# Ten chunks of several lists started after 17 routed tiles, and the chunk table computed in two parts

## The reference, cut to what matters

```python
def _moe(tokens, router_w, w1, b1, w2, b2):       # N=3125, D=256, E=8, TOP_K=2
    logits = tokens.astype(jnp.float32) @ router_w.astype(jnp.float32).T
    probs = jax.nn.softmax(logits, axis=-1)
    rw, re = jax.lax.top_k(probs, TOP_K)
    if TOP_K > 1:
        rw = rw / jnp.maximum(rw.sum(-1, keepdims=True), 1e-12)
    combine = jnp.zeros((N, E), tokens.dtype).at[jnp.arange(N)[:, None], re].set(rw)
    out = tokens
    for e in range(E):
        h = jax.nn.gelu(tokens @ w1[e] + b1[e], approximate=False)
        y = h @ w2[e] + b2[e]
        out = out + combine[:, e:e + 1] * y
    return out
...
x = x + _L0_gnn_ref(xn, src, dst, ...) + _L0_mix_ref(xn[None], ...)[0]
x = x + _L0_ffn_ref(_layernorm(x, axis=-1)[None], ...)[0]
```

## Time and profile before

| | |
|---|---|
| median of 3 runs | 435.66 (435.45, 435.66, 439.13) |
| profiled execution, own time | 435.45 |
| its span (first to last instruction) | 433.4 |
| outside the span | 2.05 |
| PE / DVE / ACT / POOL busy share of the span | 92% / 74% / 62% / 49% |
| mean granted TensorE clock | 0.976 of 2.4 GHz |

### The profile page before, as it was taken

One profiled execution on the slowest core, in us unless ns is written; L12 is line 12 of the kernel. 1 busy time (PEld: TensorE's weight loads), 2 busy tenths in 40 slices (PEclk: granted clock), 3 DMA queues, 4 the chain that ended last, 5 costly groups with the idle time before them and its releaser, 6 DMA issues.

```text
span 433.4 us, 10046 instructions
## 1 busy us (share of the span) xinstructions
PE 400.3 (92%) x3131; PEld 315.7 (73%) x3131; DVE 319.6 (74%) x785; ACT 269.5 (62%) x676; POOL 212.6 (49%) x298
## 2 busy tenths in 40 slices
PE   1989899997999999999999999778999999899995
PEld 0878687876777777777765667563999999788994
DVE  3587959968899999999916842677688887645653
ACT  1756555576788788888834525440767676566663
POOL 4124768258334455544410024365356655655565
PEclk9999999999999999999999969877999999999999
DMA  8937210007499899999997781123466665476761
GB/s 211 190 81 257 73 27 4 3 2 151 82 176 170 160 166 162 175 166 176 169 177 279 242 283 63 43 96 112 147 180 207 188 205 155 125 189 195 201 190 43
DMA packets 111828, 64.11 MB, mean 148 GB/s; under 512 B 87986, under 2 KB 102203, under 8 KB 111647
## 3 DMA queue, kind: packets, MB, share of 16 engines
q1 hardware_dynamic: 104590, 48.14, 50.4%
q0 software_dynamic: 6368, 14.47, 9.7%
q10 hardware_dynamic: 816, 0.85, 0.8%
HBM read 24.00 MB, written 21.44 MB: 105 GB/s over the span
## 4 chain that ended last, share of the span: by engine, by line
PE 40%; DVE 26%; issue 12%; POOL 7%; DMA 7%; ACT 3%; DVEq 2%; SPq 1%; POOLq 0%
PE bank L1420 5%; DVE region_c L1132 5%; DVE region_a L980 5%; PE bank L1432 4%; PE bank L1370 4%; PE bank L1463 4%; PE bank L1335 3%; DVE region_a L1293 3%; PE bank L1344 2%; PE bank L1669 2%; DVE region_a L1287 2%; POOL out L651 2%; PE bank L1680 2%; DMA out<-region_a 2%; PE bank L1582 2%
## 5 line engine op out<-in xcount | busy, mean ns | idle before, releaser
L716 ACT CAST region_a<-bank 128x500 bf16<-128x500 f32 (+1 forms) x119 | 72.4, 670 | 15.7 <-PE bank L1370 14.7
L1669 PE MATMUL bank<-region_a,region_c 128*128 128x128 f32 x496 | 65.6, 275 | 0.0
L1680 PE MATMUL bank<-region_c,region_a 128*128 128x256 f32 x248 | 64.0, 380 | 0.0
L1669 PEld LDWEIGHTS bank<-region_a,region_c 128*128 128x128 f32 x496 | 60.3, 192 | 0.1
L1132 DVE COPY region_c<-region_w 128x1026 f32 x62 | 43.2, 697 | 18.8 <-issue 18.0
L986 DVE TENSOR_TENSOR region_a<-iota,locs 128x3200 bf16<-128x3200 bf16 x25 | 54.6, 2182 | 0.0
L1370 PE MATMUL bank<-region_a 128*128 128x125 bf16 x625 | 52.9, 219 | 1.5 <-ACT region_a L716 1.4
L1370 PEld LDWEIGHTS bank<-region_a 128*128 128x128 bf16 x625 | 42.2, 101 | 13.5 <-ACT region_a L716 3.2
L625 POOL DMA_INDIRECT xs<-rows,slot_i x25 | 24.7, 989 | 53.8 <-ACT rows L760 36.7
L980 DVE TENSOR_TENSOR region_a<-iota,keys 128x3150 bf16<-128x3150 bf16 x25 | 47.5, 1900 | 0.5 <-PE bank L1370 0.4
L601 POOL TENSOR_TENSOR rows<-rows,bp 125x256 f32<-125x256 f32 x25 | 46.6, 1866 | 0.0
(11 more groups left out here) (239 smaller groups left out, 780.1 us busy)
## 6 DMA issues: line engine op xcount, KB each, us to landing
region_a<-xs_next SPq DMA_DIRECT2D x31, 259.0 KB, 2.9
region_w<-in_w SPq DMA_DIRECT2D x4, 1024.0 KB, 9.9
region_a<-xs SPq DMA_DIRECT2D x31, 131.0 KB, 2.3
rows<-in_x SPq DMA_DIRECT2D x5, 560.0 KB
xs_next<-null SPq DMA_DIRECT2D x8, 259.0 KB, 3.8
xs_next<-null SPq DMA_DIRECT2D x1, 1554.0 KB, 10.7
xs<-null SPq DMA_DIRECT2D x8, 131.0 KB, 2.7
region_q<-in_b SPq DMA_DIRECT2D x1, 1024.0 KB, 9.7
```

The source lines that it names most:

```text
L716: nc.scalar.copy(to, count_bank(n)[:, 0:w * TP].rearrange("p (c t u) -> p c t u", c=w, t=NT)).then_inc(adj_done, 1)
L1669: last = nc.tensor.matmul(hid_ps[c % 2][:, f * P:(f + 1) * P], wc[:, c % 3, k * D + f * P:k * D + (f + 1) * P], xT[:, c % 2, k * P:(k + 1) ...
L1680: last = nc.tensor.matmul(y_ps[c % 2][:, 0:D], hT[:, c % 2, f * P:(f + 1) * P], wc[:, c % 3, (2 + f) * D:(3 + f) * D], start=False, stop=( ...
```

## The change

1. The chunks that are given out early are ten instead of three, known after 17 tiles (`SURE_T`) instead of 22, and they are whole chunks of whichever lists hold them, in the order of the lists: 17 x 125 rows less 7 x 127 that may stand in part chunks leave at least ten whole ones. `whole_chunks` divides the counts by 128 behind `weigh(3)`; `sure_chunks` turns them into rows and experts behind `choose(4)`, ahead of `weigh(4)`.
2. SP waits for the scatters of 17 tiles before the first ten loads, for the first part of the table before chunks 10 to 30, and for the second part before chunks 31 to 61.
3. PE's 26 filling matmuls and the wait for 22 scatters are gone; `positions` of the last group moves behind the loop, directly ahead of `turn_rows(0)`.
4. DVE copies the weights of chunks 0 and 1 behind `weigh(4)`, of chunk 2 behind `choose(5)`, of chunk 3 behind the weighting of chunk 0.
5. The table is split by role. Part one is begun before and finished behind the weighting of chunk 0; part two is spread over seven steps behind the weighting of chunks 12 to 18 (`SECOND` = 12).
6. The two weights of a row are made by POOL (`row_weights`, behind `goals`) instead of DVE (L1290).
7. `xch` moves to its own place in `region_q`, behind `b2x`; the second result bank is `spare` instead of `h1`.

The diff, cut to the parts named here:

```diff
-SURE = -(-ROUT[-1][0] * TP // (NX - 1)) // P
+SURE_G = 3
+SECOND = 12
+SURE_T = ROUT[SURE_G][1]
+SURE = -(-(SURE_T * TP - (NX - 1) * (P - 1)) // P)
...
-        xt_ps, hid_ps, y_ps = (y0, y1), (m0, m1), (h0, h1)
+        xt_ps, hid_ps, y_ps = (y0, y1), (m0, m1), (h0, spare)
...
-            sp.wait_ge(sent, ROUT[-1][0] * 16)
+            sp.wait_ge(sent, SURE_T * 16)
             for c in range(SURE):
                 load_chunk(c)
             sp.wait_ge(table_done, 1)
-            sp.wait_ge(sent_last, (NT - ROUT[-1][0]) * 16)
-            for c in range(SURE, NCH):
+            sp.wait_ge(sent_last, (NT - SURE_T) * 16)
+            for c in range(SURE, MC):
+                load_chunk(c)
+            sp.wait_ge(table_done, 2)
+            for c in range(MC, NCH):
                 load_chunk(c)
...
+            def row_weights(c):
+                pool.wait_ge(turned_gap, c + 1)
+                nc.gpsimd.tensor_scalar(xch[:, c % XB, W_LOW:W_HIGH + 1], halves[:], turn[:, c:c + 1], 0.5, ALU.mult,
+                                        ALU.add).then_inc(weights_made, 1)
...
             goals(0)
+            row_weights(0)
             for c in range(MC):
                 if c + 1 < MC:
                     goals(c + 1)
+                    row_weights(c + 1)
                 hand_on(c)
...
+            def whole_chunks():
+                now = pos_from(SURE_T, SURE_T + 1)[0:1, 0:NX]
+                dve.wait_ge(pos_ready, SURE_G + 1)
+                chain(nc.vector.scalar_tensor_tensor(whole[:, 0, :], now, 1.0 / P, base_p[:], ALU.mult, ALU.subtract))
+                chain(nc.vector.tensor_scalar(whole[:, 0, :], whole[:, 0, :], MAGIC, -MAGIC, ALU.add, ALU.add))
+
             def sure_chunks():
+                chain(nc.vector.tensor_tensor(whole_upto[:], up_to[:], whole[:].to_broadcast([1, NX, NX]), ALU.mult))
+                nc.vector.tensor_scalar(skipped[:, 0, :], whole[:, 0, :], -float(P), float(CAP), ALU.mult, ALU.add)
+                chain(nc.vector.tensor_reduce(whole_ends[:, 0, :], whole_upto[:], AX_X, ALU.add))
...
+                nc.vector.tensor_copy(expert_i[:, 0:SURE], sure_at[:, 0, :]).then_inc(sure_known, 1)
...
                 choose(g)
+                if g == SURE_G + 1:
+                    sure_chunks()
                 if g + 2 < NR:
                     add_graph(g + 2)
+                if g == NR - 1:
+                    copy_weights(2)
                 weigh(g)
+                if g == SURE_G:
+                    whole_chunks()
                 if g == NR - 2:
-                    sure_chunks()
+                    dve.wait_ge(w_in, 80)
+                    copy_weights(0)
+                    copy_weights(1)
...
-                    link(nc.vector.scalar_tensor_tensor(xch[:, s, W_LOW:W_HIGH + 1], halves[:], turn[:, c:c + 1],
-                                                        half[:], ALU.mult, ALU.add))
+                    dve.wait_ge(weights_made, c + 1)
...
+            def second_table(part):
+                if part == 0:
+                    chunks_of(1)
+                elif part == 1:
+                    ends_of(1)
+                elif part == 2:
+                    lists_passed(1)
+                elif part == 3:
+                    chain(nc.vector.tensor_tensor(passed_by, past[:, 1, :, :], ends[:, 0:1, :].to_broadcast([1, MC, NX]),
+                                                  ALU.mult))
+                elif part == 4:
+                    chain(nc.vector.tensor_reduce(need[:], passed_by, AX_X, ALU.max))
+                    nc.vector.tensor_scalar(need_of[:], need[:], float(SURE), None, ALU.add)
+                elif part == 5:
+                    row_steps(1)
+                elif part == 6:
+                    first_rows(1)
+
+            chunks_of(0)
+            ends_of(0)
+            dve.wait_ge(xch_in[0], 16)
+            weigh_rows(0)
+            copy_weights(3)
+            lists_passed(0)
+            row_steps(0)
+            first_rows(0)
+            dve.wait_ge(table_done, 1)
+
+            for c in range(1, NCH):
+                if c == MC - 2:
+                    dve.wait_ge(table_done, 2)
+                if 1 < c < NCH - 2:
                     copy_weights(c + 2)
                 dve.wait_ge(xch_in[c % XB], (c // XB + 1) * 16)
                 weigh_rows(c)
+                second_table(c - SECOND)
...
-                positions(g)
                 if g + 1 < NR:
+                    positions(g)
                     keep_clock(spare, 3)
                     logits(g + 1)
...
-            pe.wait_ge(tkT_done, copies_to(NR))
-            keep_clock(m0, 12)
-            pe.wait_ge(pos_read, NR)
             pe.wait_ge(x2_done, NT)
-            pe.wait_ge(sent, ROUT[-1][0] * 16)
-            keep_clock(m0, 14)
+            positions(NR - 1)
             turn_rows(0)
             turn_rows(1)
             first_layer(0)
```

More of the change, by code:

```diff
@@ L1249, in _ @@
-            chain(nc.vector.tensor_scalar(nch[:], nch[:], MAGIC, -MAGIC, ALU.add, ALU.add))
-            for r2 in range(2):
-                last = nc.vector.tensor_tensor(upto[:, r2, :, :], up_to[:], nch[:, r2:r2 + 1, :].to_broadcast([1, NX, NX]),
-                                               ALU.mult)
-            chain(last)
-            chain(nc.vector.tensor_reduce(ends[:], upto[:], AX_X, ALU.add))
-            for r2 in range(2):
-                last = nc.vector.tensor_tensor(past[:, r2, :, :], ends[:, r2:r2 + 1, :].to_broadcast([1, MC, NX]),
-                                               chunk_of[:].rearrange("p (c a) -> p c a", a=1).to_broadcast([1, MC, NX]),
-                                               ALU.is_le)
@@ L1259, in _ @@
-            chain(last)
-            nc.vector.tensor_tensor(passed_by, past[:, 1, :, :], ends[:, 0:1, :].to_broadcast([1, MC, NX]), ALU.mult)
-            chain(nc.vector.tensor_reduce(expert_f[:], past[:], AX_X, ALU.add))
-            chain(nc.vector.tensor_reduce(need[:], passed_by, AX_X, ALU.max))
-            nc.vector.tensor_scalar(need_of[:], need[:], float(SURE), None, ALU.add)
-            chain(nc.vector.scalar_tensor_tensor(list_row[:, :, 0:NX], ends[:], -float(P), list_row[:, :, 0:NX],
-                                                 ALU.mult, ALU.add))
@@ L1266, in _ @@
-            chain(nc.vector.tensor_tensor(to_next[:], list_row[:, :, 1:NX + 1], list_row[:, :, 0:NX], ALU.subtract))
-            for r2 in range(2):
-                last = nc.vector.tensor_tensor(past[:, r2, :, :], past[:, r2, :, :],
-                                               to_next[:, r2:r2 + 1, :].to_broadcast([1, MC, NX]), ALU.mult)
-            chain(last)
-            chain(nc.vector.tensor_reduce(prior[:], past[:], AX_X, ALU.add))
-            for r2 in range(2):
-                last = nc.vector.scalar_tensor_tensor(first_row[:, r2, :], prior[:, r2, :], list_row[:, r2, 0:1],
-                                                      chunk_row[:], ALU.add, ALU.add)
@@ new lines, in ends_of, with lists_passed @@
+            def ends_of(r2):
+                chain(nc.vector.tensor_tensor(upto[:, r2, :, :], up_to[:], nch[:, r2:r2 + 1, :].to_broadcast([1, NX, NX]),
+                                              ALU.mult))
+                chain(nc.vector.tensor_reduce(ends[:, r2, :], upto[:, r2, :, :], AX_X, ALU.add))
+            def lists_passed(r2):
+                chain(nc.vector.tensor_tensor(past[:, r2, :, :], ends[:, r2:r2 + 1, :].to_broadcast([1, MC, NX]),
+                                              chunk_of[:].rearrange("p (c a) -> p c a", a=1).to_broadcast([1, MC, NX]),
+                                              ALU.is_le))
+                nc.vector.tensor_reduce(expert_f[:, r2, :], past[:, r2, :, :], AX_X, ALU.add)
@@ new lines, in row_steps @@
+            def row_steps(r2):
+                chain(nc.vector.scalar_tensor_tensor(list_row[:, r2, 0:NX], ends[:, r2, :], -float(P),
+                                                     list_row[:, r2, 0:NX], ALU.mult, ALU.add))
+                chain(nc.vector.tensor_tensor(to_next[:, r2, :], list_row[:, r2, 1:NX + 1], list_row[:, r2, 0:NX],
+                                              ALU.subtract))
+                chain(nc.vector.tensor_tensor(past[:, r2, :, :], past[:, r2, :, :],
+                                              to_next[:, r2:r2 + 1, :].to_broadcast([1, MC, NX]), ALU.mult))
```

91 lines of the change are left out of this document (47 added, 44 removed).

## The result

The changed kernel takes 443.03 us (median; four runs from 441.92 to 443.88) beside 436.67 us of the kernel before: 1.0134 times as long, with an interval of 1.0097 to 1.0171. The forecast was 436.2 with a range up to 440.0. So the change makes the kernel 1.0 to 1.7% slower: 6.4 us by the medians, where the sum of the forecast had 0.7 more than its starting point (435.45 to 436.15).

What follows compares the result with a forecast made beforehand. The prediction took PE to bound the chunk loop at 1.98 us a step, DVE nearly full, and the 22nd tile's scatter and load to delay its start. 435.45 - 2.5 + 3.2 gave 436.2 us, range 432.6 to 440.0.

Steps and rivals of the forecast that it cites:

- Loss 3.2: Chunks 12 to 18: table part two behind the results makes PE 3.2 us late; bounds 2.0 and 4.2.
- 4.6 - 6 x 0.18 - 0.35: Table part two: 4.6 us of pieces, less 0.18 absorbed by DVE per step and 0.35 hidden once, gives 3.2.
- Row weights on POOL: nothing on the path: First-role loop: the row weights take POOL 0.2 to 0.25 us in its idle time and delay nothing.
- Its own sign of being wrong: First-role loop: steps above 2.0 us outside the stretch with table pieces would show POOL as the bound.
- The cast of 0.56: POOL's 128x1 cast at 302.63, ending with DVE's copy; behind the 0.9 us upper bound for the row weights.
- POOL becomes the bound: Rival, first-role loop: POOL needs 1.9 to 2.3 us a chunk, stretched by DVE's copies; 4.2 more, 440.4; chance 0.13.
- the estimate of 0.44: POOL's row weights: DVE's 0.22 us becomes roughly 0.44 by the Trainium skill page's factor of about two.
- Gain 2.5: Start: chunk 6's first layer comes at 311.65 instead of 314.11, through earlier loads; bounds 1.3 and 3.7.
- all at half speed: Start: bound for PE's work up to chunk 0's first result entirely at 1.2 GHz, ending at 302.5.
- The whole gain: Rival: the loop starts as far ahead as the data, 6.4 us, and the rest is hidden; 429.1 us; chance 0.06.

Runs made afterwards that it cites:

- part one first: Changed kernel with the rest of table part one moved ahead of chunk 0's weighting: 439.07 us, 1.0057 of the kernel before.
- fillers: Changed kernel with eleven filler matmuls put back on PE around the last positions and between the turns of chunks 0 and 1: 443.27 us, 1.0151 of the kernel before.

## Why the prediction was wrong

- **Loss 3.2** (part two of the table) is the step that failed: chunks 14 to 21 lost 7.2 us. The pieces' own work was sized about rightly: 3.5 is left when the load is moved, up to 1.1 of it still the load's. What failed is that the sum 4.6 - 6 x 0.18 - 0.35 kept DVE's step as it is in the earlier trace rows, with the copy 0.28 behind the result: with a piece and a wait between them the register load is bare, 3.7 us in seven turns. It was in the earlier trace rows already: the copy at 302.46 starts 0.77 behind the last table step, where a wait stands, and the earlier trace rows have 0.28 without one. The prediction costed the instructions of a piece, and not what its last wait does to the one behind it.
- **Row weights on POOL: nothing on the path** failed too: 1.7 us. Its own sign of being wrong came, steps above 2.0 outside the table's turns. The cast of 0.56 in the earlier trace rows was weighed as an upper bound, but only as a price per instruction. The rival "POOL becomes the bound" named the mechanism and gave it 0.13; its size (4.2) was too large, since POOL paces only some of the turns. That the new step would take 0.2 to 0.25 holds where no copy meets it (0.26), and so the estimate of 0.44 was too large there; its median in the changed kernel is 0.36, its longest 0.92.
- **Gain 2.5** came out at 0.2 from the start of the span (first layer of chunk 6 at 313.90, forecast 311.65, before 314.11). Two terms of it failed. The last positions came at 294.41 and not at 293.4 (one execution each; how much of it is chance isn't settled). From there the forecast had 18.25 us to chunk 6, measured were 19.49: the clock stayed at 1.2 GHz until 303 and not 300.5, so the first result came at 303.9 instead of 301.6; the forecast's bound "all at half speed" was 302.5. A part of that is the load of chunk 1: the first layer of chunk 0, with which the forecast let PE's unbroken work begin, comes 4.2 behind the last positions and not 3.3. But the larger sum lay elsewhere: 3 us were to be had by the order of DVE's work (part one first), while fillers, which here left chunk 0 at half clock, did not change the time. That DVE would idle while table work stands behind the idle time was in the prediction, as a description and not as a price.
- **The whole gain** (429.1 for the rival that nothing eats the earlier data) was nearly reached, by another order of the same work: 430.4 us. That kernel keeps the parts of the change that the prediction costed at nothing, `xch` in its own place, the other result bank and the order of the lists, so the loss isn't theirs.

Without the first row of the table the net of the profiles is -2.27 at the start, +7.20 in the table's turns, +1.75 in the turns that POOL paces and -0.34 behind them. Not settled: why the stretch ahead of the last positions varies between executions of kernels that are alike there, by 2.7 us in the profiles without fillers (293.81 to 296.54) and 3.2 in those with them (291.83 to 295.00), and why the stretch from chunk 31 on varies by 4.2.

## What to carry to other kernels

Where a loop is full, a piece of side work costs not only its instructions: ask which register load, wait or address the next instruction needs, and whether it is still hidden beside something when the piece ends in a wait. Put such work where its engine waits anyway, whole, before the loop begins; cut up to "fit it in", it cost more here than at once. An engine with some slack is not free for small steps if each of them can meet a long instruction of a neighbour that holds it up: look for the same instruction at two durations.

## What the runs showed that was not expected

- Seven separate waits behind 0.15 us of work each cost 5.0 us on DVE; without the waits the same work costs nothing.
- Behind one copy that starts 0.4 us late, POOL went from turns with 0.53 us of idle time to turns with 0.16, and stayed there to the end of the first role: 1.98 and 2.1 us a turn from the same instructions, in two profiles.
- The last logits take 2.53 us at 1.2 GHz in some executions and 1.37 in others, and the stretch ahead of the last positions ends anywhere from 291.83 to 296.54; stages are compared from a common event on, not from the start of the span.
